# A two-layer attention kernel: layer 0 computed transposed in four accumulators, two images at the start, score rows and norm products placed ahead of the value products

## The reference

```python
# layer 0: x is (8, 256, 1024)
q = Wq x + bq;  k = Wk x + bk;  v = Wv x + bv
attn = softmax(q^T k, axis=-1)
x = gamma * (v attn^T) + x
# layer 1
h = group_norm(x, 32 groups) * norm_w + norm_b
attn = softmax((q_w h + q_b)^T (k_w h + k_b) / 16, axis=-1)
x = x + proj_w (v attn^T) + proj_b          # v = v_w h + v_b
```

## Time and profile before

| | before |
|---|---|
| median of three runs | 851.35 us (850.29 to 851.42) |
| span of the profiled execution | 852.3 us |
| tensor engine busy | 805.0 us, 94% |
| vector engine busy | 536.9 us, 63% |
| scalar engine busy | 476.2 us, 56% |
| GpSimd busy | 194.3 us, 23% |
| DMA | 18.62 MB, 22 GB/s in the mean |

### The profile page before, as it was taken

The page is one execution under the profiler, slowest core; times in us unless marked ns, Lnnn a source line. Parts: engine busy times, 40 slices in busy tenths (PEclk is TensorE's granted clock), DMA queues, the critical chain, the costliest instruction groups (busy, mean ns, idle before and its releaser), DMA issues.

```text
span 852.3 us, 11428 instructions
## 1 busy us (share of the span) xinstructions
PE 805.0 (94%) x4076; PEld 674.3 (79%) x4076; DVE 536.9 (63%) x814; ACT 476.2 (56%) x609; POOL 194.3 (23%) x181
## 2 busy tenths in 40 slices
PE   4589889999999999999999999999999999999898
PEld 3477777888877888788878888778887888887776
DVE  5645566765677665775667656776657756563482
ACT  3662865566644765557555676447655575542261
POOL 1001613040420414113330404204141133104300
PEclk9979799999999999999999999999999999999999
DMA  5000000000200001000200002000010000000001
GB/s 173 1 1 1 11 40 1 0 25 1 74 0 0 25 25 49 0 0 25 74 0 0 25 0 74 0 0 25 25 49 0 0 25 26 1 1 25 25 1 50
DMA packets 10339, 18.62 MB, mean 22 GB/s; under 512 B 2128, under 2 KB 3920, under 8 KB 10320
## 3 DMA queue, kind: packets, MB, share of 16 engines
q1 hardware_dynamic: 10320, 18.36, 6.2%
HBM read 9.97 MB, written 8.39 MB: 22 GB/s over the span
## 4 chain that ended last, share of the span: by engine, by line
PE 67%; DVE 18%; ACT 8%; issue 6%; DMA 1%; DVEq 0%; SPq 0%; ACTq 0%
PE pv_ps L477 10%; PE pv_ps L478 10%; PE pv_ps L479 10%; PE ring L477 9%; PE ring L479 9%; PE ring L478 9%; PE pt_ps L511 6%; DVE neg_raw L891 5%; ACT prob L686 3%; PE ring L496 3%; DVE x L836 2%; DVE bn L839 1%; DVE k L814 1%; DVE k L812 1%; DVE pt_lo L872 1%
## 5 line engine op out<-in xcount | busy, mean ns | idle before, releaser
L686 ACT ACTIVATE prob<-ring,neg_max 128x1024 f32<-128x1024 f32 x128 | 143.0, 1117 | 131.1 <-DVE neg_max L892 94.3
L477 PE MATMUL pv_ps<-pt_hi,v_hi 128*128 128x512 f32 x512 | 202.0, 394 | 0.5 <-DVE pt_lo L872 0.3
L478 PE MATMUL pv_ps<-pt_lo,v_hi 128*128 128x512 f32 x512 | 200.5, 392 | 0.0
L479 PE MATMUL pv_ps<-pt_hi,v_lo 128*128 128x512 f32 x512 | 200.3, 391 | 0.0
L891 DVE TENSOR_REDUCE neg_raw<-ring 128x1 f32<-128x1024 f32 x64 | 78.1, 1220 | 76.3 <-PE ring L479 72.0
L662 ACT ACTIVATE pt_hi<-prob,row_inv 128x1024 fp32r<-128x1024 f32 x64 | 73.8, 1153 | 80.6 <-DVE row_inv L879 77.3
L477 PE MATMUL ring<-h_hi,query_hi 128*128 128x512 f32 x256 | 103.1, 403 | 13.5 <-ACT prob L686 13.5
L889 DVE TENSOR_REDUCE neg_max<-ring 128x1 f32<-128x1024 f32 x64 | 78.4, 1225 | 59.2 <-PE ring L496 58.3
L477 PEld LDWEIGHTS pv_ps<-pt_hi,v_hi 128*128 128x128 f32 x512 | 96.7, 189 | 20.9 <-DVE pt_lo L872 1.1
L479 PEld LDWEIGHTS pv_ps<-pt_hi,v_lo 128*128 128x128 f32 x512 | 96.5, 188 | 21.0
L478 PEld LDWEIGHTS pv_ps<-pt_lo,v_hi 128*128 128x128 f32 x512 | 96.7, 189 | 18.5
(11 more groups left out here) (103 smaller groups left out, 1267.0 us busy)
## 6 DMA issues: line engine op xcount, KB each, us to landing
out_y<-res SPq DMA_DIRECT2D x32, 256.0 KB, 2.1
x_in<-in_x SPq DMA_DIRECT2D x7, 1024.0 KB, 4.9
x_in<-in_x SPq DMA_DIRECT2D x2, 512.0 KB, 4.9
h_f<-in_wv_t SPq DMA_DIRECT2D x1, 256.0 KB, 5.0
res<-in_wq SPq DMA_DIRECT2D x1, 256.0 KB, 5.0
res<-in_wk SPq DMA_DIRECT2D x1, 256.0 KB, 5.3
res<-in_wv SPq DMA_DIRECT2D x1, 256.0 KB, 5.5
res<-in_wp_t SPq DMA_DIRECT2D x1, 256.0 KB, 5.5
```

What stands on the lines that cost most here:

```text
L477: mm(out, w_hi, m_hi, start=first, stop=False)
L478: mm(out, w_hi, m_lo, start=False, stop=False)
L479: return mm(out, w_lo, m_hi, start=False, stop=last)
L686: activation(prob[:, k % 2], ring[:, slot], ACT.Exp, bias=neg_max[:, k % 2:k % 2 + 1], accum_out=row_sum[:, k % 2:k % 2 + 1]).then_inc(S[" ...
```

## The change

Layer 0's attention is computed transposed. First the score rows of an image (query rows by all keys, `scores`) are computed only to find, per query, the maximum and the sum of exponentials; the result is not kept, since the exponential is written back into its ring slot. Minus maximum minus logarithm of the sum is the query's shift. Eight small matmuls turn the shifts of 1024 queries into two rows (high part and remainder), which are put under the queries as partitions 96 and 97 of `q4`, with ones in `k4`. Then `keys` computes the logits again with key rows by all queries, with the shift already in them; the exponential of that is the normalised, already transposed attention. Transposes, scaling and `pt_ps` go; `q4` and `k4` are stacked on 96 partitions instead of 128 (two vector operations instead of three per half).

The freed PSUM makes `pv_ps` four accumulators, so that a tile's value products (12 matmuls of 512 columns) cover all 1024 columns in one step, two steps after the tile instead of six. Layer 1 is computed as before, row by row, in that form as well. `x_in`, `q4` and `k4` are doubled, and score rows of image i+1 are computed in turn i, image 0's ahead of everything, image 1's in turn 0. The hardware loop is gone: all turns are written out, by `turn(i)`.

```diff
+    if i == 0:
+        steps[3].sides = [("qk", 1, 0), ("qk", 1, 1)]
...
+        for k, s in enumerate((4, 5, 6, 7, 8, 8, 9, 9)):
+            steps[s].late.append(("scores", 1, k))
...
+    elif has(i + 1):
+        steps[2].sides += [("qk", i + 1, 0), ("qk", i + 1, 1)]
+        for k in range(TILES):
+            steps[6 + k].late.append(("scores", i + 1, k))
+        steps[14].log = i + 1
+        steps[15].late.append(("shift", i + 1, 0))
+    if has(i - 1):
+        steps[0].hidden = i - 1
+        for m in range(2):
+            steps[3 + m].sides.append(("query", i - 1, m))
+        for m in range(4):
+            steps[5 + m // 2].sides.append(("value1", i - 1, m))
+    if has(i + 1):
+        for m in range(4):
+            steps[10 + m].sides.append(("value0", i + 1, m))
+    if has(i):
+        for m in range(2):
+            steps[11 + m].late.append(("norm", i, m))
+    if has(i + 2):
+        steps[14].split_x = i + 2
...
+            def fill(now, entry):
+                kind, i, m = entry
+                n, slot = now.ring[entry], now.slot[entry]
+                out = ring[:, slot]
+                if n >= 2:
+                    wait(*reader(SLOT_OF[n - 2]))
...
+            for now in STEPS:
+                if now.tile:
+                    fill(now, now.tile)
+                for entry in now.sides:
+                    fill(now, entry)
+                for entry in now.late:
+                    fill(now, entry)
+                for tile in now.values:
+                    values(*tile)
```

More of the change, by code:

```diff
@@ L53 @@
 VW = C + 2
[L57 to L69, removed]
@@ L120 @@
[L120 to L126, removed]
-        self.late = []
[L128 to L133, removed]
+PROBS = 3
+PT = 4
+BANKS = CT * HALVES
+class Step:
+    def __init__(self):
+        self.tile = None
+        self.sides = []
+        self.values = []
+        self.late = []
+        self.log = None
+        self.hidden = None
+        self.split_x = None
+        self.evacuate = None
@@ L134, in __init__ @@
         self.slot = {}
+        self.ring = {}
     def entries(self):
[L137 to L146, removed]
-    t = (s - PV_LAG) % STEPS
-    part = there((t // TILES, t % TILES // 4, t % 4), 0 if s >= PV_LAG else -1)
-    step = Step(tile(0), [(kind, m) for kind, m in ITEMS.get(s, []) if has(IMAGE_OF[kind])],
-                [part] if part else [], values_first=s == VALUES_FIRST,
-                h=(s,) if s < CT and has(-1) else (), load_x=s == TILES and has(1),
-                block0=s == 2 and has(-2))
-    step.previous, step.old = tile(1), tile(2)
-    step.late = [item for item in step.items if s == 2 or item == ("norm", 0)]
-    return step
@@ L161, in take_slots @@
-def take_slots(steps, first):
-    n = first
-    for step in steps:
-        for entry in step.entries():
-            step.slot[entry] = n % 2
-            n += 1
-    return steps
-def span(*turns):
-    return [regular(lambda d: 0 <= i + d < IMAGES, s) for i, steps in turns for s in steps]
-FIRST = 3
-HEAD = span((-1, (10, 11, 12)), (0, range(STEPS)), (1, range(PV_LAG)))
-HEAD[FIRST + 14].items.insert(0, ("bias", 0))
-for _step in HEAD:
-    _step.hi_first = True
-take_slots(HEAD, 0)
-TURNS = IMAGES - 2
@@ new lines @@
+STEPS = head() + [step for i in range(IMAGES + 2) for step in turn(i)]
+SLOT_OF, TILE_NO, PHASE_NO = [], {}, {}
+for _step, _next in zip(STEPS, STEPS[1:] + [Step()]):
+    for _entry in _step.entries():
+        _step.ring[_entry] = len(SLOT_OF)
+        _step.slot[_entry] = len(SLOT_OF) % 2
+        SLOT_OF.append(_entry)
+    if _step.tile:
+        TILE_NO[_step.tile[0] == "logits", _step.tile[1], _step.tile[2]] = len(TILE_NO)
+    for _layer, _image, _k in _step.values:
+        if _k == 0:
+            PHASE_NO[_layer, _image] = len(PHASE_NO)
+        if _k == TILES - 1:
+            _next.evacuate = (_layer, _image)
```

1026 lines of the change are left out of this document (500 added, 526 removed).

## The result

| | before | after |
|---|---|---|
| median of the runs | 850.82 us (849.30 to 851.42, 4 runs) | 955.51 us (953.43 to 958.53, 4 runs) |
| ratio, 95% interval | | 1.123 [1.119, 1.126] |
| span of the profiled execution | 852.3 us | 952.5 us |

The change makes the kernel 12% slower: slower as forecast, inside the range of 880 to 965, 36 us above the predicted 920 and outside the 905 to 935 of the prediction's own case.

The account below looks back on a forecast made before the run. The tensor engine was taken to bound the kernel. A turn of 94.3 us work, 14.8 waits and 0.4 port gave 109.5; head 105, six turns 657, last turn 87 and tail 71 made 920 us, range 880 to 965.

Parts of the forecast that it names:

- step 0: A turn's first key tile waits for the scalar engine's copy of the shift row: 2.1 us.
- step 3: Wait after both halves of query/key come in one step, behind their read-outs: 2.2 us a turn.
- step 7: The second score row reuses the ring slot of the first and waits: 1.2 us a turn.
- step 10: Wait lengthened because the vector engine empties four accumulators before the row maximum: 2.8 us a turn.
- steps 11 to 13: The third ring fill of each step waits for the slot of that step's logits: 1.65 us each, 5.0 together.
- 94.1 us by count: Matmul work of a turn: transposes dropped, score-row and shift products added to the old count, old idle included; 94.1 us.
- 105 with a little for a low clock: Filling before the steady turns: turn 1 counts from 104 us, 105 with a small allowance for the clock.
- Turn 7 and the tail: Last turn, without a next image, 87 us; then remaining value steps, queries, logits and store, 71 us.
- The first (matmul count decides): Score rows in steps 10 to 13 find their slot free, only matmul work counts: 829 us, faster; chance 0.04.
- The second (the clock): The granted clock halves for a 10 us stretch each turn: 950 us, twice a turn 980; chance 0.17.
- The third (the port): Vector operations locked out by GpSimd on shared SBUF ports: 1.9 to 4 us more a turn, 932 to 944; chance 0.10.
- The fourth (half the waits): Waits of a turn are about half of those walked: 7.5 us a turn, 876 us; chance 0.05.

Follow-up runs that it names:

- the three orders of the first experiments: Changed kernel with value products before score rows, norm products and shift: 936.02 us; only norm products behind value products: 946.75; half the value products each side: 921.93.
- the version with the best turn: Changed kernel with value products halved around late fills, query/key halves in steps 1 and 2, norm products in 14 and 15, values before first key tile: 901.33 us.
- The filler: Changed kernel with four idle matmuls, their result overwritten, behind each of image 0's score rows: 950.37 us, ratio 1.115.
- the other order: Changed kernel with image 0's hidden remainders ahead of image 2's input split on GpSimd, and image 2's queries and keys two steps later: 953.74 us.
- earlier splitting: Changed kernel with the high part of image i+2's input made on the scalar engine in step 13 instead of 14: 959.41 us, ratio 1.128.

## Why the prediction was right or wrong, point by point

- **The waits: right, place by place.** Predicted and measured in the turn above: step 0, 2.1 and 2.65; step 3, 2.2 and 1.61 (0.25 + 1.36); step 7, 1.2 and 1.36; step 10, 2.8 and 2.25; steps 11 to 13, 1.65 and 1.51 each; norm products, 0.75 and 0.48 each. Together 14.8 and 13.35. The one sequence of the earlier trace rows priced three of them within 0.15 us; in step 3 and step 0 the errors of 0.6 and 0.55 have opposite signs and nearly cancel, which is luck. That the order is their cause is shown by the three orders of the first experiments: each moved or shortened the waits in front of which it put work, the first two by about what was forecast, the third by more.
- **The work of a turn: the term that failed.** "94.1 us by count" (the sum then goes on with 94.3, without a reason) became 99.6. Part of this could be read beforehand: the count for the kernel before gave 96.0 + 1.65 = 97.6 against a measured turn of 99.5, and I left out these 1.9 us. At a clock of 1.00 the work was 96.7 us in the third interval of the kernel after and 96.8 in the version with the best turn, 2.4 more than 94.3. The other 2.9 us are the half clock, as the intervals of equal work and equal waits show: 96.7 us at 1.00, 99.6 at 0.97, 101.4 at 0.96. A pair of score matmuls that starts after a wait does last 0.73 instead of 0.63, but the interval at 1.00 has all these restarts in it, so they are no part of the 2.9.
- **The turn:** 109.5 predicted. The first key tiles of turns 2 and 7 start at 230.93 and 794.35 us, so five turns took 112.7 each: 3.2 too little in my sum, 19 us over six turns. That is 2.4 for the count and 2.7 for the clock, less 1.45 of waits and 0.4 for the port, which I had added. The one interval at the full clock took 110.0, within 0.5 of the forecast, but by the errors of the count and of the waits cancelling.
- **The head: 13 us short.** Stepping one turn of 112.7 back from 230.93, turn 1 counts from 118, not 105. The first key tile came at 42.30 instead of 38 (two score rows per 3.8 us, not 3.3), and the query of image 0 at 133.14 instead of 121:

```profile
42.30 0.47 PE L391 MATMUL ring<-q,k 98*128 98x512 f32 x1 [1.31 <-ACT q L598]
...
133.14 0.77 PE L374 MATMUL ring<-h_hi,wqq_hi 128*128 128x512 f32 x1 [3.70 <-POOL h_lo L322]
```

  The step that failed is "105 with a little for a low clock". The head waits more than the turns do, and its clock was 0.73 in two of the first five stretches of 25 us, where the prediction had only "a little" for it. The filler shows 2.9 us of the lateness at the first key tile to be that clock, and up to 5.5 at the first maximum. GpSimd's queue, which I had walked as the critical chain, did hold the query's start: 7.9 us of waits were ended by it, and the other order brought the query 6.2 us forward. But work and a wait that moved behind the query took most of it back. How the rest of the 13 us divides between waits and clock stays open.
- **Turn 7 and the tail: right.** From 794.35 to the end are 158.2 us; predicted were 87 + 71 = 158. The parts fit too: image 7's first maximum was due some 112 us after the first key tile of turn 7 (87, then 24, then 1.1 for the logits) and came at 907.32, after 113.0.
- **Unrolling: right.** Every one of the ten waits of the turn above was ended by another engine, none by the supply of instructions.
- **Rivals.** The first (matmul count decides) fell: ten idle pieces a turn. The second (the clock) came true in small: a mean of 0.97 over the turn is some 7 us at half the clock, and it cost 2.9 us of the usual turn, about 15 us in the six intervals. With earlier splitting it was the full rival in every other turn. In the kernel after, each of the ten half-clock stretches of the six intervals, by the clock records of the trace, begins during a wait or within 1.1 us of its end. With the waits cut to 5.15 us a turn there were two such stretches in place of ten. The Trainium skill warns of this in TensorE: Matmul & The Clock Gate, section A second HAM failure mode: psum-queue depth-cycling, as brief idling between groups of matmuls. The trace agrees in kind, with 0.73 and 0.81 granted beside the waits. It does not show the waits to be enough for it: the third interval had them all and ran at 1.00. The third (the port) is seen in the rows, 1.95 us for remainders of 1.27, but the wait it can touch is 2.65 us against 2.1, close to the 0.4 that was taken; moving it won nothing back. The fourth (half the waits) fell: 13.35 us, of which 8.1 stand before score rows, where about 9 were forecast.

The sum so reads: 118 + 6 x 112.7 + 158 = 952, the span, against 105 + 657 + 158 = 920. The mechanism was right; the head and the work of a turn were priced too low, the latter in part by the clock, which the prediction had as a rival and not in its sum.

## What to carry to other kernels

In an in-order engine with two buffer slots, the third fill of a step waits for the reader of the first; work that could cover it must stand ahead of it, not behind, and half ahead of each of two waiting fills can be worth more than all in one place. In this kernel that was 106.5 us a turn against 109.2. Before adding counts of instructions for a new order, make the same count reproduce the old time, and carry the remainder along. To price the clock, compare repetitions of the same code that were granted different clocks. Before splitting a loss at an event, count the work that stands ahead of it on both sides. Price a straight-line head by its own waits and clock, since what is hidden in a steady turn is exposed there.

## What the hardware showed that I had not expected

- GpSimd's remainder also stops tiny vector operations: 128x8 ones, 0.17 us alone, took 1.48 and 2.33 us beside it, more than the 0.7 that a remainder of 128x1024 lost. What decides is not their size but how long the operation that they meet still runs: it was over 1.46 and 2.30 us after their starts, and 0.85 us after that of the remainder at 455.90. The remainder of the earlier trace rows fits: GpSimd's operation ran 2.11 us more, and 1.93 were lost. GpSimd pays as well: its value remainders take 1656 ns in the mean where they took 1292 before. In two turns that were looked at, those that began while a vector remainder was running took 2.10 to 2.13 us, and the others 1.28 to 1.30.

```profile
L345 POOL TENSOR_TENSOR v_lo<-v_f,v_hi 128x512 fp32r<-128x512 f32 x32 | 53.0, 1656 | 113.8 <-ACT v_hi L605 112.0
```

```profile
L371 POOL TENSOR_TENSOR v_lo<-h_f,v_hi 128x512 fp32r<-128x512 f32 x32 | 41.3, 1292 | 110.9 <-ACT v_hi L696 110.8
```

- The clock can fall at one point of a program in one turn and stay up at the same point in the next (0.83 and 1.00 above, 8 us of difference). A small edit elsewhere can go with a different pattern: executions of the kernel with the head's filler differ by 13 us, those of the kernel after by 5.
